# Another place for the next v in the longest step, its scores bank and input sums spread out, in an attention and LoRA kernel

## The reference

```python
h = layernorm(x) * (1 + ca) + sa
q, k, v = h @ Wq + bq, h @ Wk + bk, h @ Wv + bv      # 256 -> 2048, split into 16 heads of 128
attn = softmax(q @ k.T / sqrt(128)) @ v               # per batch and head, 512 x 512
x = x + ga * (attn @ Wo + bo)
h = layernorm(x) * (1 + cb) + sb
x = x + gb * (h @ W.T + lora(h))                      # 8 experts of rank 16, 2 chosen by a router
```

## Time and profile before

| | |
|---|---|
| median of 3 runs | 799.0 us (796.27 to 799.66) |
| profiled execution | 796.76 us, span 794.8 us |
| mean granted TensorE clock | 0.993 |
| PE busy | 770.1 us (97%) |
| DVE | 657.9 us (83%) |
| POOL | 625.6 us (79%) |
| ACT | 557.9 us (70%) |

### The profile page before, as it was taken

The page is one execution under the profiler, slowest core; times in us unless marked ns, Lnnn a source line. Parts: engine busy times, 40 slices in busy tenths (PEclk is TensorE's granted clock), DMA queues, the critical chain, the costliest instruction groups (busy, mean ns, idle before and its releaser), DMA issues.

```text
span 794.8 us, 15245 instructions
## 1 busy us (share of the span) xinstructions
PE 770.1 (97%) x4128; PEld 650.4 (82%) x4128; DVE 657.9 (83%) x1267; ACT 557.9 (70%) x1226; POOL 625.6 (79%) x656
## 2 busy tenths in 40 slices
PE   8998988999999999999999999999999999988998
PEld 7887776888888888888888888888888888877787
DVE  7899876879788788878888788878798788869976
ACT  4787665677777767776777777777777677676651
POOL 5478888888887987888878977888788977888932
PEclk9999998999999999999999999999999999999999
DMA  8354333443445344543455344543455344743202
GB/s 254 99 147 117 75 74 91 131 133 92 100 134 152 96 105 121 137 132 90 98 141 151 91 105 119 145 125 90 98 142 155 86 105 123 204 115 87 61 1 106
DMA packets 71703, 92.01 MB, mean 116 GB/s; under 512 B 19478, under 2 KB 36599, under 8 KB 71671
## 3 DMA queue, kind: packets, MB, share of 16 engines
q1 hardware_dynamic: 52944, 75.31, 36.7%
q10 hardware_dynamic: 18726, 16.32, 7.0%
HBM read 23.39 MB, written 2.11 MB: 32 GB/s over the span
## 4 chain that ended last, share of the span: by engine, by line
PE 52%; DVE 27%; issue 11%; SPq 4%; ACT 3%; POOL 2%; DMA 1%; DVEq 0%; ACTq 0%; POOLq 0%
PE score L1543 7%; PE score L1544 7%; PE score L1545 7%; DVE pB L1323 6%; DVE neg_max L1308 4%; DVE y_acc L1277 4%; PE o L1543 4%; PE o L1544 4%; PE o L1545 4%; SPq L436 3%; DVE u L1234 3%; DVE v_lo L1246 2%; PE y L1543 2%; DVE o_lo L1251 2%; PE qv L1543 2%
## 5 line engine op out<-in xcount | busy, mean ns | idle before, releaser
L570 POOL TENSOR_TENSOR pT_parts<-pT,pT_hi 128x512 fp32r<-128x512 f32 x248 | 318.0, 1316 | 94.0 <-ACT pT_hi L801 93.9
L870 ACT ACTIVATE prob<-score,neg_max 128x512 f32<-128x512 f32 x256 | 173.0, 687 | 82.1 <-DVE neg_max L1308 82.0
L1323 DVE STREAM_TRANSPOSE pB<-prob 128x512 f32<-128x512 f32 x252 | 161.2, 685 | 18.6 <-PE o L1545 17.3
L1308 DVE TENSOR_REDUCE neg_max<-score 128x1 f32<-128x512 f32 x256 | 158.7, 680 | 5.9 <-POOL y_acc L648 5.5
L801 ACT ACTIVATE pT_hi<-pT 128x512 fp32r<-128x512 f32 x248 | 141.4, 624 | 25.9 <-DMA pT<-pB 25.9
L1543 PE MATMUL score<-k_hi,q_hi 128*128 128x512 f32 x256 | 102.8, 402 | 9.2 <-DVE v_lo L1246 8.1
L1544 PE MATMUL score<-k_lo,q_hi 128*128 128x512 f32 x256 | 100.9, 394 | 0.0
L1545 PE MATMUL score<-k_hi,q_lo 128*128 128x512 f32 x256 | 100.4, 392 | 0.0
L1543 PE MATMUL o<-pT_hi,v_hi 128*128 128x512 f32 x248 | 99.0, 399 | 0.3 <-POOL pT_parts L570 0.3
L1544 PE MATMUL o<-pT_parts,v_hi 128*128 128x512 f32 x248 | 99.2, 400 | 0.0
L1545 PE MATMUL o<-pT_hi,v_lo 128*128 128x512 f32 x248 | 98.0, 395 | 0.0
(11 more groups left out here) (442 smaller groups left out, 1985.9 us busy)
## 6 DMA issues: line engine op xcount, KB each, us to landing
pT<-pB SPq DMA_DIRECT2D x1008, 64.0 KB, 2.0
x_nat<-in_L_attn_x_dram SPq DMA_DIRECT2D x6, 512.0 KB, 8.9
out_dram<-x_nat SPq DMA_DIRECT2D x8, 256.0 KB, 2.0
stage<-in_L_attn_wv_codes_dram ACTq DMA_DIRECT2D x7, 256.0 KB
stage<-in_L_attn_wv_scales_dram ACTq DMA_DIRECT2D x14, 128.0 KB
stage<-in_L_attn_wq_codes_dram ACTq DMA_DIRECT2D x7, 256.0 KB
stage<-in_L_attn_wq_scales_dram ACTq DMA_DIRECT2D x14, 128.0 KB
stage<-in_L_attn_wk_codes_dram ACTq DMA_DIRECT2D x7, 256.0 KB
```

Source lines behind the costliest of these rows:

```text
L570: pool.tensor_tensor(turned(par, kt, pT_lo), turned(par, kt), split(pT_hi, kt).bitcast(f32), ALU.subtract).then_inc(p_lo_ok, 1)
L870: act.activation(prob[:, i], score_ps[i][:, :], ACT.Exp, bias=neg_max[:, i:i + 1], accum_out=row_sum[:, s % 2, i:i + 1]).then_inc(exp_ok, 1)
L1308: dve.tensor_reduce(neg_max[:, i:i + 1], score_ps[i][:, :], AX.X, ALU.max, negate=True).then_inc(max_ok, 1)
L1323: dve.transpose(pB[:, s % 2, :, i].rearrange("p g k q -> p k g q"), prob[:, i].rearrange("p (k g q) -> p k g q", k=QT, g=G)).then_inc(pB_o ...
```

## The change

It has five parts, all in the order or the place of work; what is computed stays.

1. At t=0 PE now does both token tiles of the next v between product 7 and product 4; before, one tile stood on either side of product 4. At t=3 products 1 come first, then the weighted outputs, then products 2 and both v tiles. The next v waits for three exponentials of the step, no longer four.
2. v goes into score2 instead of score3, and the second half of the output projection into score3. So the third score tile waits for v_lo and the fourth for y. In steps 0 to 5 of pair 0 v goes into bank qv.
3. ACT makes v_hi earlier (at t=0 before q_hi, k_hi; at t=1, 2 before prob_high; at t=3 behind one prob_high instead of two) and DVE does v_lo ahead of y_add, at t=0 also ahead of q_lo and k_lo.
4. pB and pT are laid out so that the columns of a block of 32 of all four row tiles stand together: pT is read by PE in runs of 128, and o_hi and o_lo are put back into token order as they are read from the bank.
5. Input sums are made later and one by one: in pair 0 four are finished (DVE in steps 3 to 6), the others in steps 1 to 3 of pair 1, with their low parts on POOL behind prob_low. PE waits for each sum where its product needs it. The two memsets of y_acc move from POOL to DVE. `pair(1)` is written out in front of the loop on ACT, DVE and POOL.

The core of the diff:

```diff
@@ banks
-        v_ps = score_ps[3]
-        y_ps = [o_ps[1], score_ps[2]]
+        v_ps = score_ps[2]
+        y_ps = [o_ps[1], score_ps[3]]
@@ layout of pB and pT
         def turned(par, kt, t=None):
-            return (pT32 if t is None else t)[:, par, :, :, kt, :].rearrange("p a i q -> p i a q")
+            return (pT32 if t is None else t)[:, par, :, kt].rearrange("p a i q -> p a (i q)")
+        def in_token_order(v):
+            return v.rearrange("p (a i q) -> p i a q", a=G, i=QT)
+        def by_tile(v):
+            return v.rearrange("p (i a q) -> p i a q", i=QT, a=G)
@@ when the sums are there
+        T_SUBBED = {(0, 1): 1, (0, 2): 2, (0, 4): 3, (1, 1): 4, (0, 3): 5, (1, 3): 7, (1, 2): 8, (1, 4): 9}
+        T_DONE = {(0, 2): 1, (0, 4): 2, (0, 3): 3, (0, 1): 4, (1, 1): 5, (1, 2): 6, (1, 3): 7, (1, 4): 8}
@@ POOL first_pair
-                pool.wait_ge(t_subbed, 8)
-                for i in range(2):
-                    t = (B - 1) * QT + 2 * i
-                    pool.memset(y_acc[:, t:t + 2], 0.0).then_inc(y_zero, 1)
-                for count, i in enumerate((1, 3, 2, 4)):
-                    input_mix_lo(1, i, 5 + count)
+                input_mix_lo(0, 3)
@@ POOL pair, behind prob_low
+                    if isinstance(p, int) and p == 1 and s < 4:
+                        for pb, i in (((0, 1),), (), ((1, 1),), ((1, 2), (1, 3)))[s]:
+                            input_mix_lo(pb, i)
@@ ACT pair, t == 0
                         for m in "qk":
                             sum_kept(m, 7, u3, now)
+                        v_out(n + 2, batch_of((s + 1) % SPP) % 2, (s + 1) % 2)
                         q_high(SPP + 2 * now, 1)
                         k_high(SPP + 2 * now, 1)
-                        prob_and_v(p, s)
+                        prob_high((s - 1) % 2, landed(p, s - 1))
@@ DVE, input sums
+            def input_mix_ahead():
+                dve.tensor_tensor(t_sum(1, 4), h32[2][:, 1], h32[2][:, 0], ALU.subtract).then_inc(t_subbed, 1)
+                dve.wait_ge(t_subbed, 6)
+                for i in range(2):
+                    t = (B - 1) * QT + 2 * i
+                    dve.memset(y_acc[:, t:t + 2], 0.0).then_inc(y_zero, 1)
@@ DVE pair
                     o_low(n - 1)
+                    if isinstance(p, int) and p == 1 and 1 <= s < 4:
+                        input_mix(1, (3, 2, 4)[s - 1])
                     if t == 0:
+                        v_low(n + 2, batch_of(nxt) % 2, nxt % 2)
                         q_low(SPP + 2 * now, head_at(p, s + 1))
                         k_low(SPP + 2 * now, head_at(p, s + 1))
...
+                    if t:
+                        v_low(n + 2, batch_of(nxt) % 2, nxt % 2)
                     y_add(n - 2, batch_of(s - 2), (s - 2) % 4, False)
-                    v_low(n + 2, batch_of(nxt) % 2, nxt % 2)
@@ PE scores
-                        if i == 2 and not (first and s < 3):
+                        if i == 2 and not (first and s < SPP - 1):
+                            pe.wait_ge(v_lo_ok, n + 1)
+                        if i == 3 and not (first and s < 3):
                             pe.wait_ge(y_ok, QT * (n - 2))
-                        if i == 3:
-                            pe.wait_ge(v_lo_ok, n + 1)
@@ PE pair, t == 0
                         for m in "qk":
                             pe.wait_ge(kept_ok[m], kept("u2", now))
+                            pe.wait_ge(t_ok, T_DONE[cy, 3])
                             product(mix_ps[m], m, 7, b, False).then_inc(product_mm[m], 1)
-                        next_v_tile(p, s, 0)
+                        next_v(p, s)
                         for m, done in (("q", q_mm), ("k", k_mm)):
                             pe.wait_ge(kept_ok[m], kept("u3", now))
+                            pe.wait_ge(t_ok, T_DONE[cy, 4])
                             pe.wait_ge(w_ok[m], parts_of(m, p) + 3)
                             product(mix_ps[m], m, 4, b, False).then_inc(done, 1)
-                        next_v_tile(p, s, 1).then_inc(v_mm, 1)
                         out_projection(p, s)
```

More of the change, by code:

```diff
@@ L688, in pair @@
                     elif s == 4:
+                        if isinstance(p, int) and p == 1:
+                            input_mix_lo(1, 4)
                         block_sums("q", p + 1)
@@ L711, in pair @@
                         prob_low(n - 1, (s - 1) % 2)
+                    if isinstance(p, int) and p == 1 and s < 4:
+                        for pb, i in (((0, 1),), (), ((1, 1),), ((1, 2), (1, 3)))[s]:
+                            input_mix_lo(pb, i)
             first_pair()
-            with pool.Fori(1, PAIRS - 1) as p:
+            pair(1)
+            with pool.Fori(2, PAIRS - 1) as p:
                 pair(p)
@@ L795, in o_high, with o_high_last @@
                 act.wait_ge(o_mm, count)
-                act.activation(o_hi[:, :], bank[:, :], ACT.Copy).then_inc(o_hi_ok, 1)
+                act.activation(by_tile(o_hi[:, :]), in_token_order(bank[:, :]), ACT.Copy).then_inc(o_hi_ok, 1)
+            def o_high_last(count):
+                act.wait_ge(o_mm, count)
+                act.activation(o_hi[:, :], o_ps[0][:, :], ACT.Copy).then_inc(o_hi_ok, 1)
             def prob_high(par, have, to=pT_hi, kts=range(QT)):
-                act.wait_ge(p_land[par], have)
+                if kts:
+                    act.wait_ge(p_land[par], have)
                 for kt in kts:
@@ L1034, in pair @@
                         act.dma_start(gb_row[:, :], bass.AP(gate_dram.tensor, D, [[0, P], [2 * D, B], [1, D]])).then_inc(ld_gb, 16)
+                    if isinstance(p, int) and p == 1 and s < 4:
+                        for pb, i in (((0, 1),), ((1, 1),), ((1, 2),), ((1, 3), (1, 4)))[s]:
+                            input_mix_hi(pb, i)
                     if s == SPP - 2 and not last:
@@ L1052, in _ @@
             first_pair()
-            with act.Fori(1, PAIRS - 1) as p:
+            pair(1)
+            with act.Fori(2, PAIRS - 1) as p:
                 pair(p)
@@ L1250, in o_low, with o_low_last @@
                 dve.wait_ge(o_hi_ok, count)
-                dve.tensor_tensor(o_lo[:, :], bank[:, :], o_hi[:, :].bitcast(f32), ALU.subtract).then_inc(o_ok, 1)
+                dve.tensor_tensor(by_tile(o_lo[:, :]), in_token_order(bank[:, :]), by_tile(o_hi[:, :]).bitcast(f32),
+                                  ALU.subtract).then_inc(o_ok, 1)
+            def o_low_last(count):
+                dve.wait_ge(o_hi_ok, count)
+                dve.tensor_tensor(o_lo[:, :], o_ps[0][:, :], o_hi[:, :].bitcast(f32), ALU.subtract).then_inc(o_ok, 1)
             def bv_through_wo(p, heads=range(2)):
@@ L1449, in _ @@
             dve.wait_ge(y_zero, 2)
-            with dve.Fori(1, PAIRS - 1) as p:
+            pair(1)
+            with dve.Fori(2, PAIRS - 1) as p:
                 pair(p)
@@ L1843, in first_outputs @@
                     product(first_ps[m], m, 1, b, True).then_inc(product_mm[m], 1)
-                next_v_tile(p, s, 0)
+                weighted_ready(p, s)
+                weighted(n - 2, s % 2, batch_of(s - 2) % 2, j)
                 for m, done in (("q", q_mm), ("k", k_mm)):
@@ L1896, in first_pair @@
                         modulation_columns(2)
-                        pe.wait_ge(exp_ok, QT * (n + 1))
-                        project_v(batch_of(nxt), nxt % 2, tiles=range(1))
+                    if s < 6:
+                        pe.wait_ge(q_ok, n + 2)
+                    if s == 1:
+                        project_v(batch_of(nxt), nxt % 2, qv_ps, range(1))
                         modulation_columns(3).then_inc(mod2_mm, 1)
-                        project_v(batch_of(nxt), nxt % 2, tiles=range(1, 2)).then_inc(v_mm, 1)
+                        project_v(batch_of(nxt), nxt % 2, qv_ps, range(1, 2)).then_inc(v_mm, 1)
+                    elif s == 6:
+                        next_v(0, s)
                     else:
-                        next_v(0, s)
+                        project_v(batch_of(nxt), nxt % 2, qv_ps).then_inc(v_mm, 1)
                     if s in INPUT_AT:
```

106 lines of the change are left out of this document (52 added, 54 removed).

## The result

The changed kernel takes 803.85 us (median of 5 runs, 802.07 to 807.25) against 799.0 us. The ratio is 1.0078, with a 95% interval of 1.0057 to 1.010: slower by 5 to 6 us. The forecast was 800.0 with no difference that can be measured; the time lies in its range, and the difference is beyond the 0.5% that the forecast counted as no change.

The account below looks back on a forecast made before the run. PE bounds the steady part, busy 87.59 of 88.00 us. Terms of +0.1 through pair 1, +1.4 in the loop and +0.5 in the last pair took 796.76 to 798.8, adjusted for run spread to 800.0; range 791 to 807.

Parts of the forecast that it names:

- Start of step 7: Pair 0: PE idles about 3.6 us for v_lo but restarts at 102.0 instead of 105.22, 3.2 us won.
- What pair 1 takes back: Pair 1: PE waits for POOL's late input sums, 3.2 us in step 9 and 2.5 in step 12, plus slow clock.
- the half clock: After pair 1's new long waits TensorE runs slower, adding 1.5 us in step 9 and 0.9 in step 12.
- Rival C: Pair 1: three input mixes on DVE take 1.7 instead of 0.7 us each; 803 us in all; chance 0.10.
- the mix in step 10: Pair 1: DVE's input mix delays that step's output projection by about 0.8 us.
- small waits: Pair 1: the longer new waits swallow small ones of before, counted as -0.7 us.
- The long step: Steady part, t=0: new wait for k_lo of 0.39 us; net +0.11 per cycle, +1.4 us for 13 cycles.
- The term of 0.20 for PE's idle time: Steady part: PE's own idle time in a cycle absorbs 0.20 us of the 0.39 us wait for k_lo.
- rival B: Steady part: k_lo late in all 14 first steps, PE restarts slowly, 0.49 us each; 805.4 us; chance 0.20.
- Last pair: Fourth step and last steps: later maxima against earlier v_out and attention sums; +0.5 us net, between -1.7 and +1.0.
- The order part: Last pair, fourth step: y_add now lies between v_low and the maxima, about 1.7 us; +1.0 after v_out's 0.57 gain.
- A: Pair 1's new waits come without half clock, and the output projection hides k_lo's wait; 794.5 us; chance 0.26.

Follow-up runs that it names:

- second profile: Profile of the changed kernel, unchanged, from its repeat run; span 799.2 us, against 805.1 us in the first profiled execution.
- e11: Kernel before the change with only the new order of the longest step (t=0), v_hi and v_lo early there; 804.91 us, ratio 1.0101.
- after: The changed kernel with all parts of the change, against the kernel before; 803.85 us, ratio 1.0078.
- e2: Kernel before the change with only the new layout of pB and pT and the permuted o_hi and o_lo; 795.09 us, ratio 0.998.
- e4: Changed kernel with y_add ahead of v_lo again in the last pair's fourth step only; 804.79 us, ratio 1.009 to the kernel before.
- e13: The changed kernel, unchanged, timed and profiled once more; 803.37 us, ratio 1.0091 to the kernel before.
- e10: Changed kernel with the whole steady order put back (banks, t=0, t=3, v_hi, v_lo) and two input sums earlier; 792.08 us, ratio 0.993.
- e6: Kernel before the change with only the two memsets of y_acc moved from POOL to DVE; 797.24 us, ratio 1.0004.

## Why the prediction was right or wrong

**As a whole.** The time lies in the forecast's range, but the account of it holds only in part. By stages, in the first and the second profile: +0.8 and -0.6 us at step 13 (+0.1 expected), +2.3 and +2.5 in the loop to step 56 (1.4 for all thirteen cycles), +5.5 and +0.4 in the last pair (+0.5), +1.7 and +2.1 in the tail (0). The sum had the loop and the tail too small for both profiles, and the last pair for one.

**Start of step 7.** Right: PE waits for v_lo longer than before (3.83 us; 3.6 expected) and restarts at 101.0 (102.0), and step 9 starts at 126.2 (126.9). The last figure owes something to luck: step 8 began 3.5 us earlier than before, not 2.0, and took 13.8 us, not 13.0.

**What pair 1 takes back.** Right in place and size: 2.64 us behind POOL's sum in step 9 (3.2 expected), 2.61 in step 12 (2.5). With the half clock step 9 took 4.5 us longer than before (4.7 expected) and step 12 5.2 in one profile, 3.4 in the other (3.8 expected with 0.4 for k_lo), as the clock fell in one and not in the other. Sum at step 13: +0.8 and -0.6, expected +0.1. Rival C's price, the mixes on DVE in pair 1, wasn't paid: steps 10 and 11 took 10.1 and 12.2 us, as before. Nor were the forecast's own +0.8 for the mix in step 10 and -0.7 for small waits, two terms that cancel.

**The long step.** The wait for k_lo was right in place, in every such step, and too small: 0.59 and 0.48 us by turns from start to start instead of 0.39, and nothing of it is absorbed. Where 0.59 is lost, k_lo ends 0.35 us behind the moment at which PE could go on, just as forecast; but PE then starts 0.24 behind k_lo's end, where the forecast had 0.04. The term of 0.20 for PE's idle time was the second mistake. e11 shows 0.70 us a cycle, more than rival B's 0.49, with the slow restart that B named, 0.10. In the changed kernel it is 0.23 a cycle all the same, 0.11 expected, because only t=0 is longer, by 0.45, and t=1, 2 and 3 are shorter by 0.03, 0.09 and 0.10. The layout gives some of that (0.09 a cycle by e2). The rest, about 0.4 if such gains add, must come from the banks and the other order of t=3, ACT and DVE: about 0.1 is the pause in the third tile that e11 has and after hasn't, the remainder no run separates. Thirteen cycles make 3.0 us where the sum had 1.4.

**Last pair.** +0.5 expected, +5.5 from step 56 to 63 in the first profile and +0.4 in the second: the term holds for one execution and fails for the other. The order part, +1.0 for y_add between v_lo and the maxima, was in the sum (1.6 by e4). What wasn't is the sequence behind it: SP issues the transfer later by a varying amount, PE waits for v_lo in the third tile and not in the fourth, and over the 7 us behind that wait the clock was 0.53 after 2.90 us, 0.76 after 2.06 and 1.00 after 1.32.

**The tail.** Left out of the sum, it was 1.7 and 2.1 us longer. One of SP's issues is slow here too, in the last step: 1.54 us in the first profile and 1.85 in the second, where before has 0.59. The transfers behind it go out later, and ACT, which waits for them, starts 8.46 us into the last step before and 9.78 in e13. First before, then e13:

```profile
742.32 0.59 SPq L436 DMA_DIRECT2D pT<-pB  x1
...
746.88 0.63 ACT L801 ACTIVATE hT_hi<-pT 128x512 fp32r<-128x512 f32 x1 [0.18 <-DMA pT<-pB]
```

```profile
744.72 1.85 SPq L449 DMA_DIRECT2D pT<-pB  x1
...
750.52 0.63 ACT L819 ACTIVATE hT_hi<-pT 128x512 fp32r<-128x512 f32 x1 [1.56 <-DMA pT<-pB]
```

DVE's first subtraction behind it then takes 1.60 us instead of 0.83, which makes up the rest. Every kernel built from the changed one has such an issue in the last step, of 0.96 to 1.85 us, e10 with the old steady order among them, and a tail of 57.7 to 59.4. Before, e2, e6 and e11 have none over 0.61; the tail is 56.4 in three of them, and 57.7 in e6, for another reason (last section). So the tail's loss isn't the steady order's, nor the layout's, nor the memsets' alone; which part of the change brings the slow issue stays open.

**Rivals.** A fell: the stalls brought half clock in most cases, and k_lo's wait wasn't hidden. B had the mechanism of the long step right, but its price was not what after paid, 0.23 us a cycle; its total, 805.4, came near for other reasons, the last pair and the tail. C's total, 803, was the nearest, by luck: its mechanism wasn't there. Slower had been given 0.29, less than no difference.

## What to carry to other kernels

On an engine that is nearly always busy, a stage moved away from behind a product takes the cover from the product's consumer: reckon from the last matmul to the ready operand and compare it with the work that is left in between. If that work is too short, count the whole wait in every iteration, with the way from the operand's end to PE's next start (0.24 us here), since here the other engines' chain shifted with it. Treat banks, the order of the engine that frees them, and the order of the one that fills them as one edit: undoing the banks alone made it 8 us worse here. Move a sum out of a full stage only if it doesn't end behind a longer job in the queue of its new one. And look at the queue that issues the transfers: the one that the last pair waits for came late because it was issued late.

## What the hardware showed that was not expected

In the last pair DVE adds two SBUF tiles (x_nat) while POOL subtracts SBUF tiles (pT_parts). The kernel before and e6 have the same instructions there, yet DVE's addition took 1.70 us in one and 3.00 in the other. First before, then e6, DVE's timeline at the start of the last step:

```profile
739.36 1.70 DVE L1297 TENSOR_TENSOR x_nat<-y_acc,x_nat 128x1024 f32<-128x1024 f32 x1
741.09 2.48 DVE L1308 TENSOR_REDUCE neg_max<-score 128x1 f32<-128x512 f32 x4
```

```profile
737.97 3.00 DVE L1293 TENSOR_TENSOR x_nat<-y_acc,x_nat 128x1024 f32<-128x1024 f32 x1
741.00 2.48 DVE L1304 TENSOR_REDUCE neg_max<-score 128x1 f32<-128x512 f32 x4
```

Counted from step 63, before has DVE's addition at 0.94 and POOL's third subtraction at 1.52, which then takes 2.25 us instead of 1.29. In e6 they stand at 0.93 and 1.50: POOL's third takes 1.35, DVE's addition 3.00, and POOL's fourth 2.32. The 1.30 us pass into the tail whole. The Trainium skill, page "SBUF — State Buffer", on the shared port pair, says that whoever starts first holds it for its whole instruction and the other blocks. The trace agrees in that the losing operation grows by about the length of the other's. It doesn't agree in who loses, as far as the rows tell: the addition starts ahead of POOL's third subtraction in both kernels, and in e6 it is the addition that grows. The starts in the two kernels differ by 10 to 20 ns; what decided isn't shown.
